# Segment sums of a two-layer GNN on Trainium2: the split of counted and gathered edge tiles moves between two passes, and one-hots move from ScalarE to VectorE

## The reference, cut to what matters

```python
def sage_conv(x, edge_index, W_l, b_l, W_r, num_segments):
    src, dst = (edge_index[0], edge_index[1])
    agg = jax.ops.segment_sum(x[src], dst, num_segments=num_segments)
    return agg @ W_l.T + b_l + x @ W_r.T
h = jax.nn.relu(sage_conv(x, edge_index, W_l_in, b_l_in, W_r_in, n))
out = sage_conv(h, edge_index, W_l_out, b_l_out, W_r_out, n)
```

## Time and profile before

| | us |
|---|---|
| median of 3 runs (lowest, highest) | 3947.89 (3943.47, 3954.85) |
| the profiled execution, its own time | 3945.08 |
| its span in the trace | 3943.2 |
| set-up | 0 to 77 |
| first pass | 77 to 888 |
| node stage | 888 to 931 |
| second pass | 931 to 1675 |
| attention and the rest | 1675 to 3943 |

### The profile page before, as it was taken

How to read it: one execution, slowest core, us unless ns; L and a number is a source line. 1 busy time by engine, 2 the same in 40 slices (tenths; PEclk the granted TensorE clock), 3 DMA queues, 4 the chain that set the end, 5 groups by cost and what they waited for, 6 DMA issues and landing times. The chain is left out here.

```text
span 3943.2 us, 82423 instructions
## 1 busy us (share of the span) xinstructions
PE 2831.0 (72%) x28125; PEld 2379.0 (60%) x28125; DVE 2713.9 (69%) x7548; ACT 2489.6 (63%) x7102; POOL 2640.4 (67%) x2669
## 2 busy tenths in 40 slices
PE   3788888887888888864666866676666666667656
PEld 2666666664767777664555755565556665556644
DVE  7998767763554555462577777777776778777776
ACT  4566667765666666520367776677766786667745
POOL 3467777746555566247777777777777777777735
PEclk9899999998999999975567677677775777767767
DMA  3678884105666677532333333333333333333311
GB/s 88 245 305 340 338 313 163 21 14 202 233 214 216 233 247 238 172 112 60 81 76 89 89 87 86 77 90 88 88 83 76 89 92 83 83 82 88 85 30 39
DMA packets 285954, 536.16 MB, mean 136 GB/s; under 512 B 116631, under 2 KB 203217, under 8 KB 278902
## 3 DMA queue, kind: packets, MB, share of 16 engines
q1 hardware_dynamic: 200032, 452.07, 33.3%
q0 software_dynamic: 80256, 76.21, 10.5%
q10 hardware_dynamic: 5246, 2.56, 0.2%
HBM read 355.50 MB, written 175.09 MB: 135 GB/s over the span
## 5 line engine op out<-in xcount | busy, mean ns | idle before, releaser
L2033 POOL DMA_INDIRECT scratch<-fs_scratch,src_idx x728 | 718.0, 986 | 221.9 <-issue 221.6
L892 POOL DMA_INDIRECT gath<-x_parts,src_idx x532 | 549.9, 1034 | 262.8 <-issue 193.8
L1066 DVE TENSOR_SCALAR e_tab<-scratch,e_tab 128x700 bf16<-128x700 f16 (+8 forms) x1380 | 525.0, 422 | 244.7 <-PE sum_y_ps_c L981 221.6
L949 ACT ACTIVATE scratch<-sum_x_ps_c 128x600 int32<-128x600 f32 (+5 forms) x690 | 519.0, 769 | 263.7 <-PE sum_x_ps_c L981 210.5
L892 POOL DMA_INDIRECT gath<-y_parts,src_idx x412 | 404.1, 981 | 294.6 <-issue 121.1
L2161 ACT ACTIVATE scratch<-scratch,bias,weight 128x32 f32<-128x32 f32 x1360 | 483.8, 399 | 84.3 <-DVE bias L2231 84.3
L2075 PEld LDWEIGHTS ps_e<-fdw,scratch 128*128 128x128 f32 x3136 | 502.3, 243 | 22.8
L2075 PE MATMUL ps_e<-fdw,scratch 128*128 128x66 f32 x3136 | 486.1, 323 | 0.0
L2242 DVE SCALAR_TENSOR_TENSOR scratch<-ps_e,attn_sb 128x128 f32<-128x128 f32 x784 | 189.6, 285 | 422.2 <-PE ps_e L2075 421.1
L949 ACT ACTIVATE scratch<-sum_y_ps_c 128x700 int32<-128x700 f32 (+2 forms) x348 | 280.2, 831 | 277.6 <-PE sum_y_ps_c L981 274.0
L1006 PEld LDWEIGHTS sum_x_ps_d<-parts,scratch 128*128 128x128 f16 x7400 | 379.2, 100 | 97.8 <-ACT scratch L949 43.9
(11 more groups left out here) (363 smaller groups left out, 6254.4 us busy)
## 6 DMA issues: line engine op xcount, KB each, us to landing
count_scratch<-scratch SPq DMA_DIRECT2D x48, 3200.0 KB
scratch<-count_scratch SPq DMA_DIRECT2D x192, 800.0 KB
onehot<-rel_scratch SPq DMA_DIRECT2D x196, 256.0 KB, 3.5
scratch<-in_edge_attr_2x SPq DMA_DIRECT2D x390, 128.0 KB
fdw<-fd_scratch SPq DMA_DIRECT2D x392, 33.0 KB
scratch<-fs_scratch,src_idx POOLq DMA_INDIRECT x728
gath<-x_parts,src_idx POOLq DMA_INDIRECT x532
gath<-y_parts,src_idx POOLq DMA_INDIRECT x412
```

What stands on the lines that cost most here:

```text
L892: pool.indirect_dma_start(out=rows_in(s, t), out_offset=None, in_=table_dram, in_offset=bass.IndirectOffsetOnAxis(ap=src_idx[:, g, k:k + 1 ...
L949: act.activation(to, ps_c[u % pairs][:, :, 0:q].rearrange("p h (d a) -> p h a d", d=d), ACT.Copy).then_inc(kept, 1)
L1066: d = dve.tensor_scalar(cells[:, n % RING, i * width:(i + 1) * width], count_up[:, 0:width], head_key[:, tile:tile + 1], head_weight[:, ti ...
L2033: pool.indirect_dma_start(out=rows_of(m)[:, t, :], out_offset=None, in_=fs_dram, in_offset=bass.IndirectOffsetOnAxis(ap=src_idx[:, g, k:k ...
```

## The change

```diff
 CLASSES = ((2, 64, 64), (4, 160, 32), (6, 160, 20), (8, 144, 16), (10, 156, 12), (12, 120, 10), (14, 180, 9),
-           (16, 112, 8), (18, 56, 7))
-FIRST_TILES = 1032
+           (16, 112, 8))
+FIRST_TILES = 1096
 STORED = 48
...
-            lent, pairs = slots if read else 0, 2
+            lent, pairs = 0, 2
```

## The result

| | before | with the change |
|---|---|---|
| median us (lowest, highest), 4 runs each | 3950.76 (3943.47, 3954.85) | 3911.72 (3898.91, 3915.50) |
| ratio, 95% interval | | 0.9897 (0.9868 to 0.9927) |
| span of the profiled execution | 3943.2 | 3906.3 |
| first pass, first gather to last L1092 | 886.6 - 76.0 = 810.6 | 949.0 - 75.3 = 873.7 |
| second pass, first gather to last L1092 | 739.5 | 641.5 |

The kernel is 1.0% faster, inside the predicted range; 3897 was forecast. The first pass grew by 63 us (59 forecast), the second shrank by 98 (107 forecast).

What follows compares the result with a forecast made beforehand. PE was taken to bound both passes, waiting mostly for ACT in the second, with the gather queue next. First pass +59, second -107 and set-up -1 sum to -49 us, giving 3897 us, range 3866 to 3930.

Steps and rivals of the forecast that it cites:

- First pass, +59: First pass: 8 blocks more and 8 slots fewer make it 59 us longer, between +45 and +75.
- Eight own blocks fewer, -93: Second pass: 13 long and 20 short groups take 618.2 us instead of 711.5, saving 93 us.
- the fixed price of a group: Second pass: each long group takes 21.8 us and each short one 16.74, also after the change.
- ACT's one-hots, -56 and +30: Second pass: moving one-hots to DVE saves 56 us of PE's waits for ACT; DVE's in-order work costs 30.
- the first rival: Second pass: PE profits more, clock reaches 0.99, gathers stay 1.275 us, queue's floor of 610 us decides; 3865, chance 0.14.
- The queue, 625 us: Second pass: 468 gathers at 1.275 us, 13 us to the end and 15 us of one-hot interference total 625 us.
- the row of 1.88 us: Attention part: profile row where a gather starting just behind a one-hot's start takes 1.88 us, against a 0.986 mean.
- The second rival: Second pass: each DVE one-hot blocks one gather by 0.9 us, so the gather queue takes 663; kernel 3927, chance 0.15.
- Two equal limits, 632: Second pass: PE at 623 us and queue at 625, with four slots of buffer between, together give 632.
- The third rival: Both passes: work is only moved, an own block being worth 9 us in each; 3932, up to 3940, chance 0.08.
- the fourth: Second pass: PE waits out DVE's 2.9 us piece at each of 59 slots, +171 us; kernel 4028, chance 0.07.

Runs made afterwards that it cites:

- The split alone: The changed kernel with the second pass's one-hots back on ACT, keeping the new split of tiles; 3924.61 us, ratio 0.9935.
- the one-hots alone: The kernel before, split kept at 1032 and 1152 tiles, with only the second pass's one-hots moved to VectorE; 3844.86 us, ratio 0.9725.
- six gathers: The changed kernel with two of the eight gathers of each second-pass slot left out; 3848.71 us, ratio 0.9747.

## Why the prediction was right, and which of its steps were not

- **First pass, +59.** Measured +63, with two errors that partly cancelled, which is luck. The 8 new blocks take 69.7 us (L1092 from 879.38 to 949.05), 8.7 each, with 4 one-hots of slots among them; I had 69.4 for the blocks and 5.6 more for the slots. The first 74 blocks end 804.1 us after the first gather, 810.6 before: 12 slots fewer gave back 6.5 us, where I had 16. So the slots removed were worth 0.5 us each and not 1.0 to 1.8. The waits of PE for ACT in this pass rose from 42 to 57 us, which I had not priced.
- **Eight own blocks fewer, -93.** The split alone gave -76, with 3 us of matmuls for the added slots -79 for the blocks. The step that failed is the fixed price of a group: in the split alone the 13 long groups take 22.8 us in the mean instead of 21.8, and the short ones 17.0 instead of 16.74, 18 us together. The waits for tables rose from 26 to 38 us and are the larger part of it. The direction and the order of size were right.
- **ACT's one-hots, -56 and +30.** This is the mis-sized term. In the kernel before it is worth -102, not -26. The waits for ACT fell by 85 us in 42 groups, 2.0 each (I took 1.64); those for DVE, cells and sums together, rose by 18 us in 52 slots, 0.35 a slot (I took 0.5); and 38 us came from PE's own work at a higher clock, which I had left at 0.94 in the forecast and put into the first rival. In the change itself the waits for ACT fell to 5.1 us (20 to 30 expected), but the clock stayed at 0.946, as forecast, because the waits for gathered rows had come in.
- **The queue, 625 us.** The mechanism was right and named in advance, the price was too low: 0.47 us for each of 57 gathers that start under a one-hot, not 0.25 for each of 59 one-hots. I had let the mean of 728 gathers of the attention part speak against the row of 1.88 us. There are 93 of those one-hots beside 1564 gathers there. 69 of the gathers start under one; they take 1.26 us in the mean and the other 1495 take 0.98, which is 0.21 us for each one-hot, near the 0.25 that I took. In the changed second pass more gathers start under a one-hot, and earlier in it. Why the two streams fall together so there stays open. With 597 + 27 + 13 the queue's time is 637, near the measured 641.5. The second rival (663 to its end for every one) was too high because a gather starts anywhere under the one-hot and waits only for what is left of it. The rule of the Trainium skill, "SBUF — State Buffer", section "Who interferes with whom", says that the loser blocks, and the trace agrees, with 1.81 us for a gather that starts 0.22 us into a one-hot of 1.20.
- **Two equal limits, 632.** Near the 641.5 by luck: PE alone needs 584, not 623, and the queue 641, not 625. The error in PE's limit did not show, since only the later of the two counts, and the 7 us that I added for two equal limits covered a part of the queue's error.
- **The first rival** had the freed PE and its clock of 0.99 right for a pass that the queue does not hold (0.994 with the one-hots alone, 0.990 with six gathers), and its own "against" was right as well: the queue's room was none. The third rival (the work is only moved) is out, since the one-hots alone give 107 us, and so is the fourth: PE waits 19 us for cells at 59 slots, not 171.
- **What the forecast did not look at** is that the two halves of the split need not go together. The first half costs 60 us and nothing needs it.

## What to carry to other kernels

Before two engines' loads are shifted in one change, price each part alone and then ask what becomes the bound: here one line of the change was worth 107 us on a kernel that still had the old split, and together with the rest 39. A queue that is busy 55% of a pass and stands still for its consumer can become the bound when the consumer is freed (with 468 gathers it did, with 412 POOL still stood still for PE for 54 us), so its time without pauses (number x pitch) belongs in the sum from the start. And where an engine with many short waits is freed, its own work may get faster too: compare the busy time of the same instructions, not only the waits.

## What the runs showed of the hardware that I had not expected

- Short waits cost PE twice. With waits of at most 3.7 us each for ACT, the granted clock of the second pass was 0.936; without them 0.994, and the same 10292 matmuls were busy 38 us less. Waits for gathered rows did the like (0.946 against 0.990, 23 us at 9420 matmuls).
- A comparison on VectorE with both inputs in SBUF holds an indirect DMA that GpSimd issues behind it (52 of 57 end 0.81 to 0.87 us after the comparison): under 128x1024 in f32 1.44 us in the mean of 57, against 0.98, and under 128x512 in f16 1.28 in the mean of 24. With the iota in PSUM (57 gathers, 0.94 us), or as 128x128 f16 instructions with one tensor input (65 gathers, 0.96 us), nothing of the kind is seen. The wider f16 cells with one tensor input do hold some: 30 of 213 gathers in the first pass of the kernel before take over 1.2 us.
